# Other slots for the ropes and turns of a fused attention and mixture kernel

## The reference

```python
def attention(q, k, v, q_norm_w, k_norm_w, w_out):       # q: layernorm(x); k = v = ctx, 128 wide
    q, k = rms_norm(q, q_norm_w), rms_norm(k, k_norm_w)
    q = heads(q, 16); k = heads(k, 4); v = heads(v, 4)   # 32 wide, 4 query heads to a key head
    q, k = rope(q), rope(k)                              # x * cos + rotate_half(x) * sin
    attn = softmax(causal(q @ k.T / sqrt(32)))
    return merge(attn @ v) @ w_out.T

def ffn(x):                                              # 8 units of 256, 128 experts, top 4
    probs = softmax(x @ w_router)
    topk_p, topk_idx = top_k(probs, 4)
    basis = silu(x @ w_gate) * (x @ w_up)                # 8 units
    p = amplitudes[..., 0] ** 2 + amplitudes[..., 1] ** 2
    mix = p / (sum(p) + eps)                             # expert -> its 8 units
    out = sum over the 4: topk_w * expert_scale * (mix[expert] @ basis) @ w_down
    return out + silu(x @ shared_w_gate) * (x @ shared_w_up) @ shared_w_down

x = x + attention(layernorm(x), ctx, ctx, ...)
x = x + ffn(layernorm(x))
```

## Time and profile before

| what | us |
|---|---|
| median of 3 runs | 839.99 |
| lowest, highest | 839.25, 842.4 |
| profiled execution, span from the first to the last instruction | 839.9 |
| PE busy | 783.9 (93%) |
| DVE busy | 664.1 (79%) |
| ACT busy | 578.4 (69%) |
| POOL busy | 525.0 (63%) |

### The profile page before, as it was taken

How to read it: one execution, slowest core, us unless ns; L and a number is a source line. 1 busy time by engine, 2 the same in 40 slices (tenths; PEclk the granted TensorE clock), 3 DMA queues, 4 the chain that set the end, 5 groups by cost and what they waited for, 6 DMA issues and landing times. The chain is left out here.

```text
span 839.9 us, 15209 instructions
## 1 busy us (share of the span) xinstructions
PE 783.9 (93%) x4180; PEld 610.7 (73%) x4180; DVE 664.1 (79%) x1635; ACT 578.4 (69%) x1413; POOL 525.0 (63%) x687
## 2 busy tenths in 40 slices
PE   3768899899999999989999999989999999999998
PEld 2645566677877777767777788767777787788876
DVE  7657678789888878889888878779878787688774
ACT  3867787677777767778777677678777775654542
POOL 5547457986488646997477834997566624661561
PEclk9969699999999999999999999999999999999999
DMA  8222144445445445744454435545445435454550
GB/s 300 104 68 80 28 130 166 142 143 168 155 161 170 149 156 174 230 144 129 147 192 161 153 119 182 168 143 174 148 162 169 152 114 173 158 184 130 205 192 26
DMA packets 57051, 127.02 MB, mean 151 GB/s; under 512 B 10920, under 2 KB 28040, under 8 KB 56968
## 3 DMA queue, kind: packets, MB, share of 16 engines
q1 hardware_dynamic: 56968, 126.04, 45.5%
HBM read 107.55 MB, written 4.46 MB: 133 GB/s over the span
## 5 line engine op out<-in xcount | busy, mean ns | idle before, releaser
L1602 PE MATMUL u<-w_h,t_h 128*128 128x512 f32 x640 | 258.9, 404 | 5.3 <-POOL w_l L889 2.7
L1259 DVE TENSOR_TENSOR w_l<-w_raw,w_h 128x512 fp32r<-128x512 f32 x288 | 253.4, 907 | 0.2 <-ACT w_h L931 0.2
L1602 PE MATMUL u<-w_l,t_h 128*128 128x512 f32 x640 | 251.2, 393 | 0.0
L1602 PE MATMUL u<-w_h,t_l 128*128 128x512 f32 x640 | 251.0, 392 | 0.0
L931 ACT ACTIVATE w_h<-w_raw 128x512 fp32r<-128x512 f32 x384 | 219.2, 621 | 13.4 <-DMA w_raw<-in_w_units 13.1
L889 POOL TENSOR_TENSOR w_l<-w_raw,w_h 128x512 fp32r<-128x512 f32 x96 | 138.2, 1440 | 98.3 <-ACT w_h L931 97.5
L965 ACT ACTIVATE scores<-scores,mx 128x384 f32<-128x384 f32 (+1 forms) x224 | 128.4, 573 | 78.3 <-DVE mx L1203 77.1
L1203 DVE CUSTOM_DVE_ANT_0 scores<-s,mask_qk 128x384 f32<-128x384 f32 (+1 forms) x224 | 112.3, 503 | 45.5 <-PE s L1480 44.8
L1602 PEld LDWEIGHTS u<-w_h,t_h 128*128 128x128 f32 x640 | 120.9, 189 | 33.7 <-issue 6.1
L897 POOL TENSOR_TENSOR macc<-macc,gb 128x256 f32<-128x256 f32 x112 | 103.5, 926 | 66.4 <-DVE gb L1360 66.0
L1602 PEld LDWEIGHTS u<-w_h,t_l 128*128 128x128 f32 x640 | 120.5, 188 | 27.1
(11 more groups left out here) (151 smaller groups left out, 1196.1 us busy)
## 6 DMA issues: line engine op xcount, KB each, us to landing
w_raw<-in_w_units SPq DMA_DIRECT2D x160, 512.0 KB, 4.2
w_raw<-in_w_out_t SPq DMA_DIRECT2D x16, 512.0 KB, 5.0
w_raw<-in_shared_w_down SPq DMA_DIRECT2D x16, 512.0 KB, 4.5
q_st<-turned_h SPq DMA_DIRECT2D x232, 32.0 KB, 1.9
out<-x SPq DMA_DIRECT2D x16, 256.0 KB, 2.2
q_st<-turned_l SPq DMA_DIRECT2D x116, 32.0 KB, 1.9
x<-in_x SPq DMA_DIRECT2D x3, 1024.0 KB, 8.9
k_st<-turned_h SPq DMA_DIRECT2D x48, 32.0 KB, 1.9
```

The costliest lines, as they stand in the source:

```text
L1259: e.tensor_tensor(w_l[:, i % WR, k, :], w_raw[:, i % WR, k, :], f32(w_h[:, i % WR, k, :]), ALU.subtract).then_inc(s_wl, 1)
L1602: last = e.matmul(u_bank[n % 2][:], t[:, k, cols], ww[:, i % WR, k, :], start=(k == 0 and m == 0), stop=(k == KC - 1 and m == 2))
```

## The change

The ten tiles of a batch get places of their own instead of following spans: the second batch by `SECOND_TILES`, the third and fourth by `LATER_TILES`, both relative to `batch_slot`. In the first batch the last rope moves from slot 30 to 27. Second halves' key squares, scales and moments come some slots sooner; key stacks of first halves come two slots later and those of second halves one sooner. A stack of queries comes in the slot after its turn or after the start of the span two before, whichever is later. No instruction is added or removed.

```diff
-FIRST_TILES = dict(rope=(-34, -32, -20, -12, -7, 6, 9, 16, 23, 30), turn=(...), stack=(7, 16, 22, 28, 35))
+FIRST_TILES = dict(rope=(-34, -32, -20, -12, -7, 6, 9, 16, 23, 27), turn=(...), stack=(7, 16, 22, 28, 35))
+SECOND_TILES = dict(rope=(-19, -16, -13, -10, -7, -4, -1, 7, 12, 17), turn=(-16, -12, -9, -6, -2, 4, 8, 12, 17, 22))
+LATER_TILES = dict(rope=(-26, -19, -15, -12, -8, -5, -1, 7, 12, 17), turn=(-21, -16, -11, -8, -3, 4, 8, 12, 17, 23))
...
-QUERY = dict(rope=-3, turn=0, stack=1)
-KEYS = dict(rope=(-21, 2), turn=(-18, 5))
-
-PREP = dict(key_squares=(-39, 4, -29, -8), key_scale=(-36, 5, -26, -1), query_scale=(-35, 9, -23, 4), key_stack=(1, 13, -16, 8))
+
+PREP = dict(key_squares=(-39, 4, -29, -10), key_scale=(-36, 5, -26, -7), query_scale=(-35, 9, -23, -6), key_stack=(1, 13, -14, 7))
...
-MOMENTS = (-39, -38, 4, 7, -32, -27, -6, -1)
+MOMENTS = (-39, -38, 4, 7, -32, -27, -13, -9)
...
-            hb, i = n // NB, n % NB
-            if hb < H:
-                return FIRST_TILES[name][n]
-            if i == 0:
-                return batch_slot(hb // H) + KEYS[name][hb % H]
-            return span_slot(hb * KV + i - 3) + QUERY[name]
+            b, i = n // (H * NB), n % (H * NB)
+            return batch_slot(b) + (FIRST_TILES, SECOND_TILES, LATER_TILES)[min(b, 2)][name][i]
...
-                if s == (FIRST_TILES["stack"][u - U0] if u < H * KV else span_slot(u - 2) + QUERY["stack"]):
+                if s == (FIRST_TILES["stack"][u - U0] if u < H * KV
+                         else max(span_slot(u - 2), tile_slot(query_tile(u), "turn")) + 1):
```

More of the change, by code:

```diff
@@ L17 @@
 LEAD = dict(inverse=-1, spread=2, second_pass=4, inverse_turn=5, values=9, high=0)
-FIRST_TILES = dict(rope=(-34, -32, -20, -12, -7, 6, 9, 16, 23, 30), turn=(-17, -13, -8, -1, 6, 12, 15, 21, 27, 34), stack=(7, 16, 22, 28, 35))
+FIRST_TILES = dict(rope=(-34, -32, -20, -12, -7, 6, 9, 16, 23, 27), turn=(-17, -13, -8, -1, 6, 12, 15, 21, 27, 34), stack=(7, 16, 22, 28, 35))
+SECOND_TILES = dict(rope=(-19, -16, -13, -10, -7, -4, -1, 7, 12, 17), turn=(-16, -12, -9, -6, -2, 4, 8, 12, 17, 22))
+LATER_TILES = dict(rope=(-26, -19, -15, -12, -8, -5, -1, 7, 12, 17), turn=(-21, -16, -11, -8, -3, 4, 8, 12, 17, 23))
 THROUGH_DRAM = (5,)
```

## The result

| | before | after |
|---|---|---|
| median of 4 runs, us | 839.62 | 857.83 |
| lowest to highest | 838.75 to 842.4 | 855.39 to 859.96 |
| profiled execution: its span | 839.9 | 855.4 |

The ratio is 1.0202, 95% interval 1.0172 to 1.0233: 2% slower, where 1% faster was forecast, and outside the range of 826 to 839.5. The time of the profiled execution was 857.08 us.

A forecast was written before the change was run, and what follows sets the result against it. PE, busy 93% of 839.9 us, was taken to bound the kernel, with its costly waits on POOL as what a schedule can give back. 5.6 + 4.2 - 0.5 - 0.9 = 8.4 us gave 831.5 us, range 826 to 839.5.

The forecast's parts named there:

- part 3(d): SP's and ACT's DMA queues: stacks moved by a slot or two still land well ahead of use; cost nothing.
- Part 1: Crowded slots 101 to 108 and batch 3's like: three ropes moved out save PE 2.8 us a batch, 5.6 us.
- Rival 1: Where POOL's waits go, DVE or ACT is next in line; half the gain returns as waits: 835.0 us, chance 0.25.
- Part 2: Batch 1, slots 53 to 60: earlier ropes remove waits for POOL and the half clock behind one; 4.2 us gained.
- Part 3(a): Slots 38 to 52: earlier moments on DVE delay maxima PE waits for; 0.5 us lost, bounds 1.7 either way.
- Part 3(b): Slots 85 to 91: one more rope per batch beside DVE's routing and down products; 0.9 us lost in all.
- rival 3: Routing slots 36 to 42, 85 to 91, 133 to 139: ropes hold DVE off, PE waits; 849.0 us, chance 0.06.
- Part 3(c): Turns in slots of their own, in the ring of three short banks: nothing; an unlucky neighbour costs under 1 us.
- 3(e): Tile 9's rope from slot 30 to 27, tile 10's from 31 to 33: up to 1 us either way, nothing taken.
- What would show it: PE's waits for L849, L855 and L889 shrink, no half clock at 160 us, POOL not busy through slots 101 to 108.
- what would make it wrong: PE's waits for L1214, L1203 or L1281 grow, turns 22 to 26 wait, or half clock in slots 36 to 48, 85 to 91.

The follow-up runs named there:

- the kernel with the load first: The changed kernel with SP issuing a slot's weight chunk load ahead of the first keys' stack instead of behind it: 842.71 us, ratio 1.0018.
- the best one: The changed kernel with chunk load first, tiles 12 and 13's turns, a moment and a query scale later, three query stacks behind their loads: 833.64 us, ratio 0.9909.
- moments: The kernel before with only the second halves' moments, key squares and scales moved as in the change: 841.01 us, ratio 1.0004.
- late keys: The kernel before with only the first keys' stack of batches 2 and 3 two slots later: 855.42 us, ratio 1.0177.
- tiny DMAs: The kernel before with twelve more 128-byte DMAs on SP ahead of the load in slots 86 and 134: 860.6 us, ratio 1.0247.
- stacks: The kernel before with only the query stacks of spans 12, 20 and 28 one slot later, behind their chunk loads: 840.42 us, ratio 1.0004.
- e7_b1_old: The changed kernel with the chunk load ahead of the first keys' stack and batch 1 entirely as before the change: 846.94 us, ratio 1.0069.

## Why the prediction was wrong, point by point

**The step that failed is part 3(d), the DMA queues.** It counted right what moves (the first keys' stack two slots later, query stacks one later), asked for each moved transfer how long before its use it lands, found "eight left" and "six slots ahead", and wrote "Nothing". That answer holds for the keys' stack itself: in the kernel with the load first it comes still later, at next to no cost. The question not asked was what stands behind them. A stack is twelve issues and 7.6 us on SP; moved from slot 84 to 86, it stands right behind the queries' twelve and in front of chunk 25's load, which ACT asks for at 293.94 (298.76 less 4.82). 15.3 us of the 857.8 are this (842.5 with the stack put back), and the same move alone makes the old kernel 15 us slower. It could have been read ahead: SP's queue in the trace of before shows the rows of 0.59 us and the load at 284.99, directly behind the last query issue.

The Trainium skill has a sentence that points the other way (DMA: Bandwidth & Descriptors, section Issuing engines are not separate DMA queues): starting DMAs from several engines saves only the time to initiate them, "usually small relative to the DMA itself". For one of these it is 0.59 us beside 1.9 us to landing (the last number of the row below, from the page's DMA issues of the kernel after), but the landings overlap and the issues don't; twelve in a row are what decided here. No run here issues them from another engine.

```profile
q_st<-turned_h SPq DMA_DIRECT2D x232, 32.0 KB, 1.9
```

**Part 1, ropes out of the crowded slots: mechanism right, size near.** 2.8 us a batch were forecast. PE makes up 3.5 and 3.1 us in these slots in the kernel after, 3.6 and 3.6 in the best one (-1.7 to -5.3 and -5.1 to -8.7). Not all of it is the ropes': the moments and scales alone, with every rope at its old place, make up 1.1 and 1.2 us there (row "moments"). Rival 1 didn't come in its form, as waits on DVE or ACT in these slots that eat half of the gain. It came in another: the next in line was SP, which stays at its pace and took back 2.6 us a batch at slots 112 and 160.

**Part 2, slots 53 to 60: mechanism right, and part of the size was in the baseline's trace alone.** 4.2 us forecast. Of the 6.3 us between slots 46 and 58, 2.7 come before slot 56, where the moments alone bring 2.5; 3.6 come in slots 56 and 57, with 0.5 more in slot 60. The wait of 1.81 us is gone, and the granted clock is 1.00 from 157 to 170 us. But four kernels with batch 1's ropes at the old places (late keys, tiny DMAs, stacks, e7_b1_old) pass slots 56 and 57 by 1.5 or 1.6 us faster than the profiled execution of before, all at a granted clock of 1.00. Two of them, tiny DMAs and e7_b1_old, have the same wait of 1.8 us for `out_low` (PE's waits from 155 to 168 us, and the window of 155 to 170 us, in e7_b1_old):

```profile
PE u L1583 <- POOL o_l L852: 1.8, 1, 1.8
155.00:170.00 15.00, 12.84 (x75) 9.85 (x74) 11.97 (x34) 10.11 (x29) 14.13 (x23) 1.00 0.54 177
```

So the half clock behind this wait (1.7 us in the sum) is there in some executions (0.51 in the profile of before, 0.51 from 163 to 166 us in that of "moments") and not in others, and one trace can't price it; why is not shown. Some 2.0 us are left that every trace supports.

**Part 3(a), moments: mis-sized in its place.** 0.5 us lost was taken, with 1.7 as bound. The moments and scales alone cost 3.3 us in slots 42 to 46, but that is given back until slot 112 and the time is unchanged. With the rest of the change it is 6.6 us, at a granted clock of 0.57 from 110 to 122 us: putting two turns, a moment and a scale back gave 2.9 us in the median. The bound left out the lower clock that can follow a wait, although part 2 had just costed that for another place.

**Part 3(b) and rival 3, DVE behind the ropes:** 0.9 us taken, 18.9 us in the rival. In the best kernel the ropes stand where the change has them, and no more than 0.2 us is lost between slots 88 and 90 and 0.4 between 136 and 138. Rival 3 named the right slots in batches 2 and 3, the right sign and nearly the right size, by luck: the reason doesn't hold. PE did wait on DVE there, but DVE on ACT, ACT on a load and the load on SP.

**Part 3(c), turns:** the bound of "under 1 us" for an unlucky neighbour may be too low for the turn in slot 43, which was not tried alone. **3(e)**, tiles 9 and 10: left open; kernels with the same order up to slot 84 start slot 42 anywhere from 0.1 to 2.4 us later than before, which hides up to 1 us either way.

**What would show it** was right: L849 to 5.4 (about 6), L855 to 1.6 (1.3), L889 gone, POOL no longer busy through. So was what would make it wrong: the waits on L1203 grew from 4.1 to 6.6 us, and half clocks stand in slots 42 to 46 and behind the waits of slots 89 and 137. The forecast time, 831.5 us, is near that of the kernel in which SP's queue and the turn in slot 43 are out of the way, 833.6. That doesn't confirm the sum: this kernel has three edits that the change lacks, and the terms came out otherwise one by one.

## What to carry to other kernels

A DMA that is moved can cost little by coming late and much by standing in front: for each queue that an instruction is moved to, list what comes behind it and when that is needed, with the issue time of each (here 0.59 us, times twelve). When an engine gets through a stretch faster, look for the queue that runs at its own pace there; the gain is kept only if that queue's next deadline holds. And a load that must wait for its buffer goes behind other work in its queue, one that is ready goes in front: the same swap gave 15 us at two places and cost 5 at another. A lower clock behind a wait is priced from more than one trace: behind the same wait of 1.8 us it was there in two profiles here and not in two others.

## What was not expected of the hardware

An issue on SP takes as long for 128 bytes in 32 partitions as for 32 KB: 8.5 us for twelve of the first (one of them took 1.28 us), 7.6 us for twelve of the second. The two issues of a chunk load of 512 KB each take 1.05 us together in most rows, less per issue than a stack's.
